# Five layer norms: the apply goes from VectorE to ScalarE, epsilon and shift to GpSimd

## The chip, the cores and the metric

The kernel runs on one core of one Trainium2 chip. Its engines are TensorE (PE in the profile, with weight loads as PEld), VectorE (DVE), ScalarE (ACT), GpSimd (POOL) and SyncE (SP, which here only issues transfers). The metric is the time of one execution on the device in microseconds; lower is better.

## The reference

The inputs are 32 sequences of 128 tokens with 256 features, `x`, and as many context tokens. The block is a gated decoder layer and a gated feed-forward:

```python
x = x + tanh(g_xattn) * xattn(layernorm(x), ctx)      # norm 0 is this layernorm
x = x + tanh(g_ffn) * ffn(layernorm(x))               # norm 4

def xattn(x, ctx):
    x = ln(x + mha(x, x, x))        # norm 1, with gain and bias; 16 heads of 16
    x = ln(x + mha(x, ctx, ctx))    # norm 2
    f = relu(x @ w1 + b1) @ w2 + b2
    return ln(x + f)                # norm 3

def layernorm(x): return (x - mean(x)) / sqrt(var(x) + 1e-5)
```

`ffn` is a SiLU-gated product with ternary weights, whose input is rounded to 8 bits by the maximum of each token's row. Each norm is taken over the 256 features of a token.

## The kernel before

The 32 sequences go in 16 groups of two (`G = 2` slots b), each slot a tile of 128 tokens by 256 features. A group passes five stages, each in another iteration of one software pipeline: `Ap` and `A` (self attention, norms 0 and 1), `Bp` and `B` (cross attention, norm 2), `C` (the inner feed-forward, norm 3) and `E` (the ternary one, norm 4). One iteration therefore works on several groups at once, and 20 iterations do all. Iterations 0 to 4 are written out, 5 to 15 are a loop, and the rest are written out again. In the first three the ternary weights are also prepared.

`SCHEDULE` is one list of steps that all engines walk through. Each engine issues its own part of a step at that step's place, in order, and waits on semaphores for what others must do first. An engine therefore can't pass a step whose input is late, though the next one may be ready. The stretches that matter here read, in the schedule's words:

- `("O", -1), ("E", "norm"), ("W", -1), ("smax", 1, 2), ("in", "B", "K"), ("N", -1), ("Bp", "Q"), ("E", "TQ")`: norm 4 of one group stands between output steps of stage B. `W` is the output projection with the residual and the statistics of norm 1 or 2, `N` its apply.
- `("E", "GU", 0, 2), ("Ap", "norm"), ("scores", 0, 1), ("M", 1)`: norm 0 of a new group stands ahead of the scores of an attention unit. `scores` on ACT is two exponentials (`e` in float32, `ehi` in float16), on POOL their difference `elo`; `M` sends the row maxima, as `mT`, through a transfer into `stk`, whose last rows then take part in the score products.
- `("scores", 3, 1), ("smax", 4, 3), ("E", "DN", 1, 2), ("W", 2), ("M", 4), ("C", "apply"), ("Ap", "V"), ("setup", 3), ("N", 2)`: the end of an iteration. `smax` takes row maxima (`nm`) on DVE.

Queries and keys leave for DRAM (`parts`) and come back in another layout (`stk`), by transfers that SP issues; TensorE's `smax` steps wait for them. SP too goes in order: at `("Ap", "norm")` it waits for norm 0 before it loads the next `x_a`, and the transfer of `mT` stands behind that.

A norm n goes, before: DVE takes `bn_stats` and `bn_aggr` (mean and variance in `lmv`), then adds epsilon (`lve`); POOL raises that to -0.5 (`lrs`); DVE subtracts the mean and multiplies by `lrs` in one instruction for each slot (`normalize`). For norms 1 to 3 POOL then multiplies by the gain (`tg`) and adds the bias (`h`).

Of the kernel before, what the change touches and what calls it, by code (L numbers as in the profile page):

```python
# [30 lines left out]
P = 128  # L31
# [170 lines left out]
def build(nc, x, ctx_in, mask_x, mask_s, g_x, g_f, w, out):  # L202
    with ExitStack() as stack:
# [3 lines left out]
        def sem(name):  # L207
            return stack.enter_context(nc.semaphore(name))
# [143 lines left out]
        ln_aggr = {n: sem(f"ln_aggr{n}") for n in range(5)}  # L352
        ln_eps = {n: sem(f"ln_eps{n}") for n in range(5)}
        ln_rstd = {n: sem(f"ln_rstd{n}") for n in range(5)}
        ln_out = {n: sem(f"ln_out{n}") for n in range(5)}
# [66 lines left out]

        N_CONST = 12
        N_DVE = 15
# [373 lines left out]
        def _(eng):  # L798
# [19 lines left out]
            def ternary(m, part):  # L818
# [6 lines left out]
                if part == 1:  # L825
                    eng.wait_ge(u_tc, 7 * m + 3)
                    eng.activation(tq[:, :], raw[10 + m], ACT.Identity, scale=sw[:, m:m + 1], bias=magic_col[:, 0:1]).then_inc(u_tq, 1)

            def prep(st_, s, name):
                g = st_.g[{"A": "Ap", "B": "Bp"}.get(s, s)]  # L830
                if name == "norm":

                    eng.wait_ge(q_small, g.at(5, 5))
                    wait(eng, *st_.full("E", "TQ", back=1))
                    for b in range(G):
                        a_ = eng.activation(q1m[:, b, :], h4[:, b, :], ACT.Identity, scale=s1[:, b:b + 1],  # L836
                                            bias=magic_col[:, 0:1])
                    a_.then_inc(q_ready, 1)
                    return
# [49 lines left out]
            def unit_step(st_, what, k, hf=0):  # L889
                s, b, g, turn = st_.unit(k)  # L890
                if what == "scores":
# [15 lines left out]
            def iteration(st_):  # L907
                for step in SCHEDULE:
# [6 lines left out]
                    if what in ("scores", "M", "O"):  # L915
                        unit_step(st_, *step)
                    elif name in ("GU", "DN", "Q2"):
                        beside(st_, *step)
                    elif what in STAGE and name not in ("F2", "stats", "apply") and step != ("Ap", "norm"):
                        prep(st_, STAGE[what], name)  # L920
# [14 lines left out]
        def _(eng):  # L935
# [98 lines left out]
            def stats(n, g, calls, call, slots, src):  # L1034

                for k in slots:
# [6 lines left out]
                i_.then_inc(ln_aggr[n], 1)  # L1043
                eng.wait_ge(ln_aggr[n], g.at(calls, call + 1))
                a, b = slots[0], slots[-1] + 1
                eng.tensor_scalar(lve[n][:, a:b], lmv[n][:, a:b, 1], EPS, None, ALU.add).then_inc(ln_eps[n], 1)  # L1046

            def normalize(n, g, calls, call, slots, src, dst):
                eng.wait_ge(ln_rstd[n], g.at(calls, call + 1))
                for k in slots:  # L1050
                    i_ = eng.tensor_scalar(dst(k), src(k), lmv[n][:, k, 0:1], lrs[n][:, k:k + 1], ALU.subtract, ALU.mult)  # L1051
                i_.then_inc(ln_out[n], 1)

            def first_norm(st_):
# [3 lines left out]
                wait(eng, *st_.full("A", "T", back=1))  # L1058
                wait(eng, hres_in["A"], g.at(16))
                normalize(0, g, 1, 0, range(G), lambda k: x_a[:, k, :], lambda k: hin["A"][:, k, :])  # L1060

            def prep(st_, s, name):
                g = st_.g[{"A": "Ap", "B": "Bp"}.get(s, s)]
                if name == "norm":

                    eng.wait_ge(x1_ready, g.at(1, 1))
                    stats(4, g, 1, 0, range(G), lambda j: x1[:, j, :])
                    wait(eng, q_ready, g.at(1))
                    normalize(4, g, 1, 0, range(G), lambda j: x1[:, j, :], lambda j: h4[:, j, :])
                    eng.wait_ge(ln_out[4], g.at(1, 1))  # L1070
# [43 lines left out]
            def unit_step(st_, what, k, part=0):  # L1114
# [30 lines left out]
                elif what == "W":  # L1145

                    bank, fill, drain, before, after = st_.job(s, ("W", k))
                    eng.wait_ge(fill, after)
                    eng.wait_ge(hres_in[s], g.at(16, 16))
                    eng.scalar_tensor_tensor(res[s][:, b, :], bank[:, 0:D], 1.0 / WS, hres[s][:, b, :], ALU.mult,  # L1150
                                             ALU.add).then_inc(drain, 1)
                    eng.wait_ge(drain, after)
                    stats(LN_OF[s], g, G, b, range(b, b + 1), lambda i: res[s][:, i, :])
                elif what == "N":
                    wait(eng, ln_gain[LN_OF[s]], g.at(G, b))
                    normalize(LN_OF[s], g, G, b, range(b, b + 1), lambda i: res[s][:, i, :], lambda i: nrm[s][:, i, :])

            def beside(st_, s, kind, k=0, j=0):
                g = st_.g[s]
                if kind == "F2":  # L1160
                    bank, fill, drain, before, after = st_.job("C", ("F2", k))
                    eng.wait_ge(fill, after)
                    eng.wait_ge(ln_bias[2], g.at(G, k + 1))
                    eng.scalar_tensor_tensor(res["C"][:, k, :], bank[:, 0:D], 1.0 / (WS * WS), hin["C"][:, k, :],
                                             ALU.mult, ALU.add).then_inc(drain, 1)
# [3 lines left out]
                if kind == "apply":  # L1169
                    wait(eng, ln_gain[3], g.at(1))  # L1170
                    normalize(3, g, 1, 0, range(G), lambda j: res["C"][:, j, :], lambda j: nrm["C"][:, j, :])
                if kind == "GU":
# [32 lines left out]
            def iteration(st_):  # L1205
                for step in SCHEDULE:
# [6 lines left out]
                    if what in ("smax", "values", "O", "W", "N"):  # L1213
                        unit_step(st_, *step)
                    elif step == ("Ap", "norm"):
                        first_norm(st_)
                    elif name in ("F2", "stats", "apply", "GU", "DN", "Q2"):
                        beside(st_, *step)
# [15 lines left out]
        def _(eng):  # L1234
# [14 lines left out]
            const(eng.memset(ones16[:, :], 1.0))  # L1249
            const(eng.memset(neghalf[:, :], -0.5))  # L1250
            const(eng.memset(magic_col[:, :], MAGIC))
            const(eng.memset(brows[:, :], 0.0))
# [123 lines left out]
```

## Time and profile before

| | |
|---|---|
| time, median of 3 runs | 1311.1 us (1307.93 to 1313.27) |
| profiled execution, span | 1305.9 us (its time outside the span isn't recorded) |
| busy: TensorE, DVE, ACT, POOL | 72%, 69%, 43%, 42% of the span |
| mean granted TensorE clock | 0.880 |

The span is from the first to the last instruction of the one execution that the profiler recorded. A busy share is a mean over the whole span. All other times of this document that are no medians are read from that execution.

### The profile page before, as it was taken

How to read it: one execution, taken by the hardware profiler on the slowest of the kernel's cores; microseconds unless marked ns; L12 is line 12 of the kernel's file. 1: busy time of each engine (PE TensorE's matmuls, PEld its weight loads, DVE VectorE, ACT ScalarE, POOL GpSimd, SP SyncE). 2: the span in 40 equal slices, each digit the busy share in tenths (PEclk: the TensorE clock that was granted, in tenths of full speed). 3: DMA queues.
4: the chain of work that ended last, by engine and by line, in shares of the span. 5: the costliest groups of instructions: out<-in, count | busy, mean ns of one | idle time of the engine just before them, and what ended most of it. 6: DMA issues, size and time to landing. Idle time of an engine off the chain costs nothing.

```text
span 1305.9 us, 28843 instructions
## 1 busy us (share of the span) xinstructions
PE 941.4 (72%) x10103; PEld 737.1 (56%) x10147; DVE 902.5 (69%) x2063; ACT 561.7 (43%) x836; POOL 549.1 (42%) x468
## 2 busy tenths in 40 slices
PE   1254567868778787878787778797878778786674
PEld 1133445646666665656665657575756666564452
DVE  8544356558787877787878788686868787666544
ACT  2212243435444554545455445453535454542432
POOL 5012134453535454444536354535453545460510
PEclk9866677979898989898999999898999898988886
DMA  4523442424444444453544425243534444404000
GB/s 139 121 81 49 78 55 42 84 40 77 64 74 75 73 73 73 57 89 53 93 53 78 64 68 75 54 81 55 86 48 76 65 65 74 66 10 66 17 9 8
DMA packets 136288, 85.07 MB, mean 65 GB/s; under 512 B 10632, under 2 KB 131631, under 8 KB 136240
## 3 DMA queue, kind: packets, MB, share of 16 engines
q1 hardware_dynamic: 136240, 84.43, 38.2%
q8 instruction: 31, 0.51, 0.2%
q14 instruction: 17, 0.14, 0.1%
HBM read 54.49 MB, written 20.98 MB: 58 GB/s over the span
## 4 chain that ended last, share of the span: by engine, by line
PE 27%; DVE 21%; DMA 18%; issue 16%; POOL 10%; ACT 4%; SPq 3%; DVEq 1%; POOLq 0%; ACTq 0%
DMA stk_AQ<-parts_AQ 9%; PE lin_A L583 4%; PE lin_E L583 3%; DMA parts_AQ<-qk_AQ 3%; DMA stk_BQ<-parts_BQ 3%; PE lin_B L583 3%; PE smax L659 3%; SPq L476 3%; POOL lrs L1268 2%; DVE nm_A L1119 2%; PE smax L655 2%; PE st L685 2%; DMA parts_BQ<-qk_BQ 2%; PE lin_B L752 2%; DMA stk_AQ<-mT_A 2%
## 5 line engine op out<-in xcount | busy, mean ns | idle before, releaser
L1283 POOL TENSOR_TENSOR elo<-e,ehi 128x1024 f16<-128x1024 f32 x128 | 272.6, 2130 | 303.4 <-ACT ehi L896 302.8
L894 ACT ACTIVATE e<-st 128x1024 f32<-128x1024 f32 x128 | 131.0, 1024 | 190.5 <-PE st L685 190.4
L1268 POOL TENSOR_TENSOR lrs<-lve,neghalf 128x1 f32<-128x1 f32 (+1 forms) x112 | 70.0, 625 | 333.8 <-DVE lve L1046 332.2
L1119 DVE TENSOR_REDUCE nm_A<-smax 128x4 f32<-128x512 f32 x128 | 87.8, 686 | 81.3 <-PE smax L659 80.9
L896 ACT ACTIVATE ehi<-st 128x1024 f16<-128x1024 f32 x128 | 130.9, 1022 | 0.0
L655 PE MATMUL smax<-mb,ident_big 128*128 128x512 f16 x128 | 57.6, 450 | 101.5 <-DMA stk_AQ<-parts_AQ 73.7
L1119 DVE TENSOR_REDUCE nm_B<-smax 128x4 f32<-128x512 f32 x128 | 87.7, 685 | 20.1 <-PE smax L659 19.8
L659 PE MATMUL smax<-stk_BK,stk_BQ 126*128 126x128 f16 x512 | 51.7, 225 | 45.2 <-DMA stk_BQ<-parts_BQ 40.9
L655 PEld LDWEIGHTS smax<-mb,ident_big 128*128 128x128 f16 x128 | 13.2, 103 | 112.8 <-issue 54.2
L659 PEld LDWEIGHTS smax<-stk_BK,stk_BQ 126*128 126x128 f16 x512 | 35.1, 100 | 60.3 <-issue 24.7
L875 ACT ACTIVATE late<-late,magic_col,s 128x1024 f32<-128x1024 f32 x32 | 39.7, 1240 | 60.8 <-DVE s L1195 60.8
L680 PE MATMUL st<-mbT,ident_big 128*128 128x512 f16 x128 | 54.0, 422 | 6.0 <-DMA stk_AQ<-mT_A 5.1
L659 PEld LDWEIGHTS smax<-stk_AK,stk_AQ 126*128 126x128 f16 x512 | 45.9, 110 | 21.7 <-issue 10.4
L659 PE MATMUL smax<-stk_AK,stk_AQ 126*128 126x128 f16 x512 | 57.9, 243 | 0.0
L836 ACT ACTIVATE late<-late,magic_col,s 128x256 f32<-128x256 f32 x32 | 17.5, 592 | 90.5 <-DVE kap L1080 90.5
L685 PEld LDWEIGHTS st<-stk_AQ,stk_AK 128*128 128x128 f16 x512 | 43.2, 106 | 21.3 <-issue 7.4
L685 PE MATMUL st<-stk_AQ,stk_AK 128*128 128x128 f16 x512 | 53.6, 231 | 0.0
L583 PE MATMUL lin_E<-hT_C,w 128*128 128x256 f16 x384 | 50.6, 272 | 0.0
L619 PE MATMUL lin_E<-ident,late 128*128 128x128 f32 x64 | 12.2, 321 | 51.2 <-ACT late L836 51.2
L699 PE MATMUL av<-vhi_B,ehi 128*128 128x17 f16 x512 | 45.6, 172 | 3.0 <-POOL elo L1283 3.0
L1051 DVE TENSOR_SCALAR h<-x_a,lmv,lrs 128x256 f32<-128x256 f32 x32 | 37.4, 1209 | 14.5 <-POOL lrs L1268 14.5
L685 PE MATMUL st<-stk_BQ,stk_BK 128*128 128x128 f16 x512 | 44.5, 237 | 2.6 <-DVE mw L1011 1.3
(281 smaller groups left out, 3006.0 us busy)
## 6 DMA issues: line engine op xcount, KB each, us to landing
stk_AK<-parts_AK SPq DMA_DIRECT2D x64, 128.0 KB, 4.7
stk_AQ<-parts_AQ SPq DMA_DIRECT2D x64, 128.0 KB, 7.0
stk_BK<-parts_BK SPq DMA_DIRECT2D x64, 128.0 KB, 4.4
stk_BQ<-parts_BQ SPq DMA_DIRECT2D x64, 128.0 KB, 4.6
x_a<-in_x_dram SPq DMA_DIRECT2D x16, 256.0 KB, 2.8
cx<-in_ctx_dram SPq DMA_DIRECT2D x16, 256.0 KB, 2.8
parts_AK<-qk_AK SPq DMA_DIRECT2D x16, 256.0 KB, 2.3
parts_AQ<-qk_AQ SPq DMA_DIRECT2D x16, 256.0 KB, 2.9
```

The costliest lines, as they stand in the source:

```text
L583: mm = eng.matmul(dst, lhs(a, k), rhs(b, k), start=(start and at == 0), stop=(at == last))
L655: eng.matmul(smax[:, :], ident_big[:, :], mb[:, :].unsqueeze(1).to_broadcast([P, 4, P]), start=True, stop=True)
L659: mm = eng.matmul(smax[:, i * P:(i + 1) * P], stk[s, "Q"][0:XROW, h, tok], stk[s, "K"][0:XROW, h, tok], start=(s == "B"), stop=True, skip_ ...
L680: eng.matmul(st[:, k2 * 512:(k2 + 1) * 512], ident_big[:, :], mbT[:, :].unsqueeze(1).to_broadcast([P, 4, P]), start=True, stop=True)
L685: mm = eng.matmul(st[:, col:col + P], stk[s, "K"][:, h, tok], stk[s, "Q"][:, h, tok], start=(s == "B"), stop=True, skip_group_check=True)
L699: eng.matmul(dst, ehi[:, hf, i * P:(i + 1) * P], vhi[s][:, b, h, :], start=True, stop=False, skip_group_check=True)
L875: eng.activation(q2m[:, :], z2[:, :], ACT.Identity, scale=s2[:, 0:1], bias=magic_col[:, 0:1]).then_inc(q2_ready, 1)
L894: eng.activation(e32[:, hf, :], st[:, :], ACT.Exp, scale=SCORE).then_inc(e32_ready, 1)
L896: eng.activation(ehi[:, hf, :], st[:, :], ACT.Exp, scale=SCORE).then_inc(st_drained, 1)
L1119: eng.tensor_reduce(nm[s][:, 4 * part:4 * part + 4], smax[:, :].rearrange("p (h k) -> p h k", h=4), AX_X, ALU.max, negate=True).then_inc(s ...
L1268: eng.tensor_tensor(lrs[n][:, a:b], lve[n][:, a:b], neghalf[:, 0:b - a], ALU.pow).then_inc(ln_rstd[n], 1)
L1283: eng.tensor_tensor(elo[:, hf, :], e32[:, hf, :], ehi[:, hf, :], ALU.subtract).then_inc(elo_ready, 1)
```

## The change

Three pieces of a norm move, for all five norms:

- DVE keeps `bn_stats` and `bn_aggr` only. The epsilon step goes to POOL as a `tensor_tensor` add with a column of epsilons.
- POOL takes four dependent steps where it took one: epsilon (`lve`), power (`lrs`), mean times `lrs` (`lmr`), and that times -1 (`lnm`), each waiting for the one before through a semaphore.
- The apply becomes an ACT instruction, scale `lrs` and bias `lnm`, at the step's place in ACT's order.

Added waits keep a new set of statistics or a new residual from overwriting what the last apply still reads. The pieces of the diff below are, in order: the new columns, ScalarE, VectorE, GpSimd.

```diff
+        negone = sb("negone", [P, 4], F32)
+        eps_col = sb("eps_col", [P, 4], F32)
...
+            def normalize(n, g, calls, call, slots, src, dst):
+                eng.wait_ge(ln_rstd[n], g.at(calls, call + 1))
+                for k in slots:
+                    i_ = eng.activation(dst(k), src(k), ACT.Identity, scale=lrs[n][:, k:k + 1], bias=lnm[n][:, k:k + 1])
+                i_.then_inc(ln_out[n], 1)
...
+                if name == "norm" and s == "A":
+                    wait(eng, *st_.full("A", "T", back=1))
+                    wait(eng, hres_in["A"], g.at(16))
+                    normalize(0, g, 1, 0, range(G), lambda k: x_a[:, k, :], lambda k: hin["A"][:, k, :])
+                    return
                 if name == "norm":
-
+                    wait(eng, q_ready, g.at(1))
+                    normalize(4, g, 1, 0, range(G), lambda j: x1[:, j, :], lambda j: h4[:, j, :])
                     eng.wait_ge(q_small, g.at(5, 5))
...
+                if kind == "apply":
+                    wait(eng, ln_gain[3], g.at(1))
+                    normalize(3, g, 1, 0, range(G), lambda j: res["C"][:, j, :], lambda j: nrm["C"][:, j, :])
+                    return
...
+                elif what == "N":
+                    wait(eng, ln_gain[LN_OF[s]], g.at(G, b))
+                    normalize(LN_OF[s], g, G, b, range(b, b + 1), lambda i: res[s][:, i, :], lambda i: nrm[s][:, i, :])
...
             def stats(n, g, calls, call, slots, src):
-
+                wait(eng, ln_rstd[n], g.back(1).at(calls, call + 1))
...
-                eng.wait_ge(ln_aggr[n], g.at(calls, call + 1))
-                a, b = slots[0], slots[-1] + 1
-                eng.tensor_scalar(lve[n][:, a:b], lmv[n][:, a:b, 1], EPS, None, ALU.add).then_inc(ln_eps[n], 1)
-
-            def normalize(n, g, calls, call, slots, src, dst):
-                eng.wait_ge(ln_rstd[n], g.at(calls, call + 1))
-                for k in slots:
-                    i_ = eng.tensor_scalar(dst(k), src(k), lmv[n][:, k, 0:1], lrs[n][:, k:k + 1], ALU.subtract, ALU.mult)
-                i_.then_inc(ln_out[n], 1)
...
             def power(n, g, calls, call, slots):
 
+                eng.wait_ge(ln_aggr[n], g.at(calls, call + 1))
+                a, b = slots[0], slots[-1] + 1
+                eng.tensor_tensor(lve[n][:, a:b], lmv[n][:, a:b, 1], eps_col[:, 0:b - a], ALU.add).then_inc(ln_eps[n], 1)
                 eng.wait_ge(ln_eps[n], g.at(calls, call + 1))
-                a, b = slots[0], slots[-1] + 1
-                eng.tensor_tensor(lrs[n][:, a:b], lve[n][:, a:b], neghalf[:, 0:b - a], ALU.pow).then_inc(ln_rstd[n], 1)
+                eng.tensor_tensor(lrs[n][:, a:b], lve[n][:, a:b], neghalf[:, 0:b - a], ALU.pow).then_inc(ln_pow[n], 1)
+                eng.wait_ge(ln_pow[n], g.at(calls, call + 1))
+                eng.tensor_tensor(lmr[n][:, a:b], lmv[n][:, a:b, 0], lrs[n][:, a:b], ALU.mult).then_inc(ln_shift[n], 1)
+                eng.wait_ge(ln_shift[n], g.at(calls, call + 1))
+                eng.tensor_tensor(lnm[n][:, a:b], lmr[n][:, a:b], negone[:, 0:b - a], ALU.mult).then_inc(ln_rstd[n], 1)
```

What stands in a row now is shown at three places. A row is a line of the kernel, an operation, what it writes and reads, and its shape.

On ACT in iteration 4, from the norm of stage E to the maxima of the next unit, there stood before (`late<-late,magic_col,s` is the 8-bit rounding `q1m`, `late<-lin_E,hcg` a tanh of the gate):

```order
L836 ACTIVATE late<-late,magic_col,s 128x256 x2
L866 ACTIVATE qk_BQ<-lin_B 128x512
L843 ACTIVATE q1T<-lin_E 128x512
L883 ACTIVATE late<-lin_E,hcg 128x512
L866 ACTIVATE hT_C<-lin_B 128x512
L883 ACTIVATE late<-lin_C,hcg 128x512
L894 ACTIVATE e<-st 128x1024
L896 ACTIVATE ehi<-st 128x1024
L901 ACTIVATE mT_A<-lin_A 32x128
```

and now:

```order
L838 ACTIVATE late<-late,lnm,lrs 128x256 x2
L854 ACTIVATE late<-late,magic_col,s 128x256 x2
L838 ACTIVATE nrm_B<-res_B,lnm,lrs 128x256
L884 ACTIVATE qk_BQ<-lin_B 128x512
L861 ACTIVATE q1T<-lin_E 128x512
L905 ACTIVATE late<-lin_E,hcg 128x512
L884 ACTIVATE hT_C<-lin_B 128x512
L905 ACTIVATE late<-lin_C,hcg 128x512
L838 ACTIVATE h<-x_a,lnm,lrs 128x256 x2
L916 ACTIVATE e<-st 128x1024
L918 ACTIVATE ehi<-st 128x1024
L926 ACTIVATE mT_A<-lin_A 32x128
```

Three applies came in: that of norm 4 ahead of the rounding, that of norm 2 between the rounding and the copies `qk_BQ` and `q1T`, and that of norm 0 between a tanh and the exponentials `e` and `ehi`.

On POOL in the same stretch, from the split of the keys of B to the next `elo`, there stood before:

```order
L1274 TENSOR_TENSOR qk_BK<-qf_B,qk_BK 128x512
L1268 TENSOR_TENSOR lrs<-lve,neghalf 128x2
L1268 TENSOR_TENSOR lrs<-lve,neghalf 128x1
L1290 TENSOR_TENSOR tg_B<-nrm_B,lng 128x256
L1298 TENSOR_TENSOR h<-tg_B,lnb 128x256
L1268 TENSOR_TENSOR lrs<-lve,neghalf 128x2
```

and now:

```order
L1293 TENSOR_TENSOR qk_BK<-qf_B,qk_BK 128x512
L1281 TENSOR_TENSOR lve<-lmv,eps_col 128x2
L1283 TENSOR_TENSOR lrs<-lve,neghalf 128x2
L1285 TENSOR_TENSOR lmr<-lmv,lrs 128x2
L1287 TENSOR_TENSOR lnm<-lmr,negone 128x2
L1281 TENSOR_TENSOR lve<-lmv,eps_col 128x1
L1283 TENSOR_TENSOR lrs<-lve,neghalf 128x1
L1285 TENSOR_TENSOR lmr<-lmv,lrs 128x1
L1287 TENSOR_TENSOR lnm<-lmr,negone 128x1
L1309 TENSOR_TENSOR tg_B<-nrm_B,lng 128x256
L1317 TENSOR_TENSOR h<-tg_B,lnb 128x256
L1281 TENSOR_TENSOR lve<-lmv,eps_col 128x2
```

Each single power became four steps; nothing else changed places.

On DVE at the end of an iteration, between two row maxima `nm_A`, there stood before:

```order
L1138 TENSOR_TENSOR o_B<-av,rsum 128x256
L1051 TENSOR_SCALAR nrm_A<-res_A,lmv,lrs 128x256
L1119 TENSOR_REDUCE nm_A<-smax 128x4
L1143 TENSOR_TENSOR oT_B<-lin_B,oT_B 128x256
L1119 TENSOR_REDUCE nm_A<-smax 128x4
L1126 TENSOR_SCALAR nm_A<-nm_A 128x16
```

The row of L1051 is gone there, and with it all others of that line on DVE.

## Rows read from the trace of the kernel before

**Rows 1.** The page, section 1: busy time, share of the span, instructions.

```profile
PE 941.4 (72%) x10103; PEld 737.1 (56%) x10147; DVE 902.5 (69%) x2063; ACT 561.7 (43%) x836; POOL 549.1 (42%) x468
```

**Rows 2.** Timeline of TensorE, three waits for `stk_AQ`: start, length, [idle before <-releaser].

```profile
267.16 0.61 PE L655 MATMUL smax<-mb,ident_big 128*128 128x512 f16 x1 [5.81 <-DMA stk_AQ<-parts_AQ]
...
680.25 0.39 PE L655 MATMUL smax<-mb,ident_big 128*128 128x512 f16 x1 [4.34 <-DMA stk_AQ<-parts_AQ]
...
1092.31 0.60 PE L655 MATMUL smax<-mb,ident_big 128*128 128x512 f16 x1 [4.30 <-DMA stk_AQ<-parts_AQ]
```

**Rows 3.** Timeline of TensorE, DVE and POOL, 617 to 628 us, by start.

```profile
617.16 0.39 PE L659 MATMUL smax<-stk_AK,stk_AQ 126*128 126x128 f16 x4
617.30 2.34 DVE L1051 TENSOR_SCALAR nrm_A<-res_A,lmv,lrs 128x256 f32<-128x256 f32 x1
617.36 2.13 POOL L1283 TENSOR_TENSOR elo<-e,ehi 128x1024 f16<-128x1024 f32 x1 [0.95 <-ACT ehi L896]
...
619.56 0.68 DVE L1119 TENSOR_REDUCE nm_A<-smax 128x4 f32<-128x512 f32 x1
...
621.20 2.12 POOL L1283 TENSOR_TENSOR elo<-e,ehi 128x1024 f16<-128x1024 f32 x1
...
623.62 0.23 PE L669 MATMUL lin_C<-ident,nm_A 128*32 128x128 f16 x1 [1.07 <-DVE nm_A L1128]
...
627.44 0.68 DVE L1090 TENSOR_TENSOR hT_B<-lin_E,hT_B 128x512 f16<-128x512 f32 x1
```

**Rows 4.** Groups by line and shape: busy us, mean ns of one, idle before.

```profile
L1268 POOL TENSOR_TENSOR lrs<-lve,neghalf 128x1 f32<-128x1 f32 x64 | 35.9, 561 | 209.9 <-DVE lve L1046 209.9
L1268 POOL TENSOR_TENSOR lrs<-lve,neghalf 128x2 f32<-128x2 f32 x48 | 34.0, 709 | 123.9 <-DVE lve L1046 122.4
...
L1290 POOL TENSOR_TENSOR tg_A<-nrm_A,lng 128x256 f32<-128x256 f32 x32 | 23.2, 725 | 12.8 <-DVE nrm_A L1051 12.8
...
L1307 POOL TENSOR_TENSOR late<-late,lng 128x512 f32<-128x512 f32 x16 | 20.3, 1267 | 2.7 <-DVE late L1051 2.7
...
L836 ACT ACTIVATE late<-late,magic_col,s 128x256 f32<-128x256 f32 x32 | 17.5, 592 | 90.5 <-DVE kap L1080 90.5
...
L1250 POOL MEMSET neghalf<- 128x4 f32 x1 | 0.1, 101 | 0.1
```

**Rows 5.** Timeline of DVE, POOL and ACT, 636 to 641 us, by start.

```profile
636.12 0.73 DVE L1051 TENSOR_SCALAR late<-late,lmv,lrs 128x256 f32<-128x256 f32 x2 [0.89 <-POOL lrs L1268]
...
638.48 1.09 ACT L836 ACTIVATE late<-late,magic_col,s 128x256 f32<-128x256 f32 x2 [5.29 <-DVE kap L1080]
...
639.27 0.18 DVE L1042 BATCH_NORM_AGGREGATE lmv<-lst 128x2 f32<-128x6 f32 x1
...
639.72 0.54 POOL L1268 TENSOR_TENSOR lrs<-lve,neghalf 128x1 f32<-128x1 f32 x1 [3.71 <-DVE lve L1046]
...
640.37 0.41 DVE L1051 TENSOR_SCALAR nrm_B<-res_B,lmv,lrs 128x256 f32<-128x256 f32 x1
...
640.77 0.60 ACT L843 ACTIVATE q1T<-lin_E 128x512 bf16<-128x512 f32 x1 [0.72 <-PE lin_E L619]
```

**Rows 6.** Timeline of ACT, DVE, TensorE and SP, 645 to 654 us, by start.

```profile
645.15 1.02 ACT L894 ACTIVATE e<-st 128x1024 f32<-128x1024 f32 x1 [0.21 <-PE st L685]
...
646.78 0.15 DVE L1042 BATCH_NORM_AGGREGATE lmv<-lst 128x2 f32<-128x6 f32 x1
646.97 0.25 ACT L901 ACTIVATE mT_A<-lin_A 32x128 f16<-32x128 f16 x1
...
648.03 2.45 DVE L1051 TENSOR_SCALAR h<-x_a,lmv,lrs 128x256 f32<-128x256 f32 x2 [0.90 <-POOL lrs L1268]
...
651.02 0.40 PE L659 MATMUL smax<-stk_BK,stk_BQ 126*128 126x128 f16 x4 [2.06 <-DMA stk_BQ<-parts_BQ]
651.19 0.72 SPq L489 DMA_DIRECT2D stk_AQ<-mT_A  x1
...
653.76 0.39 PE L680 MATMUL st<-mbT,ident_big 128*128 128x512 f16 x1 [0.36 <-DMA stk_AQ<-mT_A]
```

More of the change, by code:

```diff
@@ L325, in build @@
         lrs = [sb(f"lrs{n}", [P, G], F32) for n in range(5)]
+        lnm = [sb(f"lnm{n}", [P, G], F32) for n in range(5)]
+        lmr = [sb(f"lmr{n}", [P, G], F32) for n in range(5)]
         carrier = sb("carrier", [1, 1], F32)
@@ L353, in build @@
         ln_eps = {n: sem(f"ln_eps{n}") for n in range(5)}
+        ln_pow = {n: sem(f"ln_pow{n}") for n in range(5)}
+        ln_shift = {n: sem(f"ln_shift{n}") for n in range(5)}
         ln_rstd = {n: sem(f"ln_rstd{n}") for n in range(5)}
@@ L914, in iteration @@
                         continue
-                    if what in ("scores", "M", "O"):
+                    if what in ("scores", "M", "O", "N"):
                         unit_step(st_, *step)
@@ L918, in iteration @@
                         beside(st_, *step)
-                    elif what in STAGE and name not in ("F2", "stats", "apply") and step != ("Ap", "norm"):
+                    elif name == "apply":
+                        beside(st_, *step, 0)
+                    elif what in STAGE and name not in ("F2", "stats"):
                         prep(st_, STAGE[what], name)
@@ L1057, in first_norm @@
                 stats(0, g, 1, 0, range(G), lambda k: x_a[:, k, :])
-                wait(eng, *st_.full("A", "T", back=1))
-                wait(eng, hres_in["A"], g.at(16))
-                normalize(0, g, 1, 0, range(G), lambda k: x_a[:, k, :], lambda k: hin["A"][:, k, :])
             def prep(st_, s, name):
@@ L1067, in prep @@
                     stats(4, g, 1, 0, range(G), lambda j: x1[:, j, :])
-                    wait(eng, q_ready, g.at(1))
-                    normalize(4, g, 1, 0, range(G), lambda j: x1[:, j, :], lambda j: h4[:, j, :])
                     eng.wait_ge(ln_out[4], g.at(1, 1))
@@ L1149, in unit_step @@
                     eng.wait_ge(hres_in[s], g.at(16, 16))
+                    wait(eng, ln_out[LN_OF[s]], g.back(1).at(G, b + 1))
                     eng.scalar_tensor_tensor(res[s][:, b, :], bank[:, 0:D], 1.0 / WS, hres[s][:, b, :], ALU.mult,
@@ L1153, in unit_step @@
                     stats(LN_OF[s], g, G, b, range(b, b + 1), lambda i: res[s][:, i, :])
-                elif what == "N":
-                    wait(eng, ln_gain[LN_OF[s]], g.at(G, b))
-                    normalize(LN_OF[s], g, G, b, range(b, b + 1), lambda i: res[s][:, i, :], lambda i: nrm[s][:, i, :])
             def beside(st_, s, kind, k=0, j=0):
@@ L1163, in beside @@
                     eng.wait_ge(ln_bias[2], g.at(G, k + 1))
+                    wait(eng, ln_out[3], g.at(1))
                     eng.scalar_tensor_tensor(res["C"][:, k, :], bank[:, 0:D], 1.0 / (WS * WS), hin["C"][:, k, :],
@@ L1168, in beside @@
                     stats(3, g, 1, 0, range(G), lambda b: res["C"][:, b, :])
-                if kind == "apply":
-                    wait(eng, ln_gain[3], g.at(1))
-                    normalize(3, g, 1, 0, range(G), lambda j: res["C"][:, j, :], lambda j: nrm["C"][:, j, :])
                 if kind == "GU":
@@ L1212, in iteration @@
                         continue
-                    if what in ("smax", "values", "O", "W", "N"):
+                    if what in ("smax", "values", "O", "W"):
                         unit_step(st_, *step)
@@ L1216, in iteration @@
                         first_norm(st_)
-                    elif name in ("F2", "stats", "apply", "GU", "DN", "Q2"):
+                    elif what == "N" or name == "apply":
+                        continue
+                    elif name in ("F2", "stats", "GU", "DN", "Q2"):
                         beside(st_, *step)
@@ L1250, in _ @@
             const(eng.memset(neghalf[:, :], -0.5))
+            const(eng.memset(negone[:, :], -1.0))
+            const(eng.memset(eps_col[:, :], EPS))
             const(eng.memset(magic_col[:, :], MAGIC))
```

2 lines of the change are left out of this document (1 added, 1 removed).

## The prediction

> **What bounds the kernel now.** I read the page's first section, then the TensorE waits on a transfer, then the timeline of one period engine by engine. The first shows that no engine is full: TensorE 941.4 us of 1305.9, VectorE (DVE) 902.5, ScalarE (ACT) 561.7, GpSimd (POOL) 549.1 [rows 1]. The bound is a chain through queues that each run in a written order. The second shows its beat: once a period TensorE waits some 4.3 us for the transfer of `stk_AQ`. From 267.16 to 1092.31 there are 12 such periods, (1092.31 - 267.16) / 12 = 68.8 us each [rows 2]. That wait is resolved by a DMA that itself answers to work earlier in the period, so whatever delays the middle of a period delays the next one's start. I follow one period, from 610 to 680 us.
>
> **Prices.** Removed from DVE: 160 applies (5 norms, 16 groups, 2 slots) and 112 epsilon adds. An apply is 0.41 us when nothing disturbs it, a pair 0.73 [rows 5], but 2.34 us at 617.30 and 2.45 a pair at 648.03 [rows 3, 6]: in rows 3 it began at 617.30, POOL's `elo` ran 617.36 to 619.49, and it ended at 619.64. Added to ACT: the same applies. The nearest row is `q1m`, also 128x256 with two column operands, 0.592 us [rows 4] and 1.09 for a pair [rows 5], so one costs 0.18 more than on DVE, a pair 0.36 more, and the next ACT instruction starts 0.50 after each.
>
> Added to POOL: three small steps per call beside the power. No row shows a small add or multiply there. Below, the cheapest POOL instruction, a memset of four columns, is 0.10; above, the power itself is 0.56 on one column [rows 4]. Between them the straight line through its products, 0.725 at 256 columns and 1.267 at 512, meets zero columns at 0.725 - 0.542 = 0.18. I take 0.20, because that row is the same instruction with a cheap operation. The hand-over between two dependent POOL instructions I estimate at 0.13 (bounds 0.08 and 0.17).
>
> The chain from the aggregate to the scale was: aggregate ends 639.27 + 0.18 = 639.45, power starts 639.72, so 0.27 for the DVE epsilon and its hand-overs [rows 5]. New: a hand-over of 0.10, then three times (0.20 + 0.13), so 1.09. Each norm's chain grows by X = 1.09 - 0.27 = 0.82 us (bounds 0.10 + 3 x 0.18 - 0.27 = 0.37 and 0.10 + 3 x 0.73 - 0.27 = 2.02).
>
> **The sum over one period.** First what is won. Without `nrm_A` at 617.30 the row maximum that starts at 619.56 can start at about 617.6, when its product is done (617.16 + 0.39), and the max transposes of 623.62 come about 2 us earlier [rows 3]. Half of that is lost at once: `nrm_B` now stands on ACT ahead of the copy of `hT_B`, and its scale waits for POOL's `elo`, which ends at 621.20 + 2.12 = 623.32. Then hand-over 0.10, epsilon 0.20, power 0.56 and two more small steps with three hand-overs of 0.13: 624.97. ACT applies at 625.07, the copy starts 0.50 later and ends at 626.17, and DVE's half of `hT_B` starts at 626.2 where it started at 627.44 [rows 3]. Gain 1.25 us, which the next steps (keys, values, output of B) carry, since each waits for the one before.
>
> Then what is paid. (a) The norm ahead of the feed-forward, on two slots: X + 0.36 = 1.18. So `q1m` moves from 638.48 to 638.48 - 1.25 + 1.18 = 638.41 [rows 5]. (b) `nrm_B` of that place stands on ACT between `q1m` and the copies `qk_BQ` and `q1T`. Its aggregate ends at 639.45 - 0.07 = 639.38; 0.10 + 0.20 + 0.13 + 0.56 + 0.13 + 0.20 + 0.13 + 0.20, and 0.10 to reach ACT, is 1.75: 641.13. Two starts of 0.50 later `q1T` starts at 642.13, where it started at 640.77 [rows 5]: the period is now 1.36 late, and TensorE's gate and up products behind it. (c) The norm of `x_a` follows these on DVE: its aggregate ends at 646.93 + 1.36 = 648.29. The chain on two columns (power 0.709 [rows 4]) takes 1.80, and 0.10 to ACT: 650.19. There the pair stands ahead of the exponentials `e` and `ehi` of another unit, which need nothing from it: `e` starts 1.0 later, at 651.19 instead of 645.15, and `mT_A`, 1.82 behind it (646.97 - 645.15), at 653.01 [rows 6]. Before, the transfer that carries `mT_A` was held on SP behind the load of `x_a`, which waits for this very norm (648.03 + 2.45 = 650.48), and was issued at 651.19. Now the norm ends at 651.3, but `mT_A` at 653.26, and the transfer goes at about 653.3. The scores waited 653.76 - 651.19 = 2.57 for it, so they start at 655.9: 2.1 us late [rows 6]. Queued behind the held ACT instructions are also the two feed-forward copies and `hT_A`; all are done before the late scores, so they add nothing.
>
> From there to the next `stk_AQ` wait no norm is on the path (`nrm_A` of the other slot costs ACT 0.5 us shortly ahead of TensorE's wait of 4.3, which absorbs it), so I let the 2.1 us stand. 12 x 2.1 = 25 us. At the ends I count +5 us, an estimate: the first norm and the last four feed-forward norms pay 1.18 each (5.9), the drain's two B applies about 1.0 each, and the relief of 1.25 comes back in two of its iterations; in the fill I let relief and stall cancel. In all +30: 1305.9 + 30 = 1336 us of span. The profiled execution shows its span alone; the median of the runs is 1311.1, so 5.2 us lie around it or are scatter, and the forecast for the median is **1341 us**.
>
> A rule that bears on the relief: the Trainium skill, "SBUF — State Buffer", section "SBUF: two separate sides", says that GpSimd and a VectorE instruction that uses both ports of the shared pair exclude each other for a whole instruction. The end of `nrm_A` 0.15 us behind `elo` agrees [rows 3]. If instead whatever DVE does next were held as long, the 1.25 us would be lost and the period 3.3 us late: 12 x 3.3 + 5 = 45, so 1356 us.
>
> **Rivals.** *The relief carries, and the waits on ACT are covered (faster).* For it: TensorE waits 2.06 us for `stk_BQ` at 651.02 in this stretch, and the old `x_a` norm took 2.45 us on DVE [rows 6]. Then every period keeps the 1.25: -15 + 5 = -10, 1301 us. It decides where `mT_A` leaves ACT by 651.19 - 1.25 = 649.9, so with the pair started by 646.9. Against it: even with the whole relief the aggregate ends at 645.7 and the chain gives 647.5.
>
> *It evens out.* With X at its lower bound the four chains of a period give back 4 x 0.45 = 1.8 of the 2.1: 12 x 0.3 + 2, so 1317 us. For it speaks only the memset.
>
> *A small POOL step costs what the power costs.* X = 2.02, so 4 x 1.2 = 4.8 more per period: 12 x 6.9 + 12 = 95, 1406 us. For it: the two rows on one and two columns are 0.561 and 0.709, and both are mostly fixed time [rows 4]. Against it: at that fixed time 256 columns could not take 0.725.
>
> **How the numbers follow.** Measured runs of this kernel spread over 0.4%, so about 0.5% (6.6 us) can be told from no change. Chances: the forecast, 1318 to 1365, 0.63; dear POOL steps, above 1365, 0.12; evened out, within 6.6 us, 0.10; relief carried, faster, 0.15. So faster 0.15, same 0.10, slower 0.75. The range 1304 to 1385 leaves out most of the faster case and the far half of the dear one.
>
> **What would show it.** Of the changed kernel: DVE busy below 780 us (902.5 - 160 x 0.41 - stretches); ACT near 650 us; small POOL steps near 0.2 us; between `tanh` and `e` on ACT a wait of some 4 us for the shift of `x_a`; a period near 71 us; `nrm_A` gone from the gap between two row maxima. I am wrong if the small steps cost over 0.4 us, if the 2 us won near 618 us reach the period's end, or if TensorE's granted clock falls in the longer waits.

## The result, and the profile after

| | before | after |
|---|---|---|
| time, median | 1309.5 us (1301.9 to 1313.3, 4 runs) | 1331.3 us (1330.1 to 1334.4, 4 runs) |
| span of the profiled execution | 1305.9 us | 1332.6 us |
| mean granted TensorE clock | 0.880 | 0.868 |

The change makes the kernel slower: the ratio is 1.0175, with a 95% interval of 1.0128 to 1.0221. Forecast were 1341 us and slower.

The page's first section of the changed kernel, which answers to [rows 1]:

```profile
PE 950.0 (71%) x10103; PEld 742.0 (56%) x10147; DVE 760.7 (57%) x1791; ACT 638.4 (48%) x996; POOL 610.0 (46%) x806
```

DVE lost 142 us of work (902.5 to 760.7), ACT gained 77, POOL 61, and TensorE is busy almost as long as before. The span grew all the same: the freed engine was not the bound.

TensorE's wait for `stk_AQ` in the timeline of the changed kernel, answering to [rows 2]:

```profile
265.70 0.61 PE L661 MATMUL smax<-mb,ident_big 128*128 128x512 f16 x1 [6.29 <-DMA stk_AQ<-parts_AQ]
...
1112.71 0.58 PE L661 MATMUL smax<-mb,ident_big 128*128 128x512 f16 x1 [4.23 <-DMA stk_AQ<-parts_AQ]
```

Twelve periods lie between the two rows: (1112.71 - 265.70) / 12 = 70.58 us each, where it was 68.76. So the 26.7 us of span are 12 x 1.82 = 21.8 in the periods, -1.5 ahead of the first row (267.16 before), and +6.3 behind the last (1332.6 - 1112.71 = 219.9, before 1305.9 - 1092.31 = 213.6).

The prices, from POOL's and ACT's groups by line and shape (busy us, mean ns of one, idle before), answering to [rows 4]:

```profile
L1283 POOL TENSOR_TENSOR lrs<-lve,neghalf 128x1 f32<-128x1 f32 x64 | 34.7, 543 | 5.0
...
L1285 POOL TENSOR_TENSOR lmr<-lmv,lrs 128x1 f32<-128x1 f32 x64 | 12.1, 190 | 5.0
L1281 POOL TENSOR_TENSOR lve<-lmv,eps_col 128x1 f32<-128x1 f32 x64 | 12.1, 190 | 188.4 <-DVE lmv L1069 188.4
```

```profile
L838 ACT ACTIVATE nrm_B<-res_B,lnm,lrs 128x256 f32<-128x256 f32 x32 | 19.2, 600 | 47.0 <-POOL lnm L1287 47.0
L838 ACT ACTIVATE h<-x_a,lnm,lrs 128x256 f32<-128x256 f32 x32 | 17.5, 593 | 66.3 <-POOL lnm L1287 66.3
```

A small POOL step costs 0.19 us, an ACT apply 0.60. The idle time in the last column says where ACT now stands still: 66.3 us in all ahead of the norm of `x_a`, 47.0 ahead of `nrm_B`, both waiting for POOL's last step. ACT's timeline of one such place, answering to [rows 6]:

```profile
727.95 1.09 ACT L838 ACTIVATE h<-x_a,lnm,lrs 128x256 f32<-128x256 f32 x2 [3.31 <-POOL lnm L1287]
728.94 1.00 ACT L916 ACTIVATE e<-st 128x1024 f32<-128x1024 f32 x1
729.85 1.01 ACT L918 ACTIVATE ehi<-st 128x1024 f16<-128x1024 f32 x1
730.75 0.25 ACT L926 ACTIVATE mT_A<-lin_A 32x128 f16<-32x128 f16 x1
```

The two exponentials and the copy of `mT_A` queue behind the applies of `h`, as forecast.

One period is a poor guide here, so the tables below are means over ten: a period begins where SP issues the transfer `parts_AQ<-qk_AQ`, the last ten intervals between such issues are taken (from 66.8 to 70.1 us in the kernel before), and a number is the mean start of the instruction behind that issue. They are worked out from the timelines of the engines.

```
mean start in the period, us                 before   after   difference
first row maximum behind stk_AQ (DVE)         13.27   13.27      0.00
third row maximum (DVE)                       20.23   19.17     -1.06
copy of the first mT_A (ACT)                  24.13   23.43     -0.70
hT_B, DVE's half                              27.96   27.51     -0.45
maximum behind norm 4 (DVE)                   37.34   37.76     +0.42
q1T (ACT)                                     40.85   42.84     +1.99
e queued behind h (ACT)                       45.61   52.15     +6.54
transfer of the second mT_A (SP)              51.32   54.24     +2.92
e of the scores that need it (ACT)            55.32   57.53     +2.21
period                                        68.59   70.81     +2.22
```

The column on the right is the forecast's walk through a period, measured: a gain at the row maxima that shrinks, three losses, and nothing after the scores.

### The profile page after: what moved, and what is told of

Read it like the earlier page. It is cut to its first block, busy times and chain, and to the rows that moved or that the text cites. A ratio compares the mean times of both kernels' runs of the same rounds, so it can differ in the third digit from the quotient of the medians.

```text
span 1332.6 us, 29220 instructions
## 1 busy us (share of the span) xinstructions
PE 950.0 (71%) x10103; PEld 742.0 (56%) x10147; DVE 760.7 (57%) x1791; ACT 638.4 (48%) x996; POOL 610.0 (46%) x806
## 4 chain that ended last, share of the span: by engine, by line
PE 28%; DMA 17%; DVE 16%; POOL 15%; issue 12%; ACT 10%; SPq 2%; ACTq 0%; DVEq 0%; POOLq 0%
DMA stk_AQ<-parts_AQ 9%; POOL elo L1302 5%; PE lin_A L589 4%; POOL lrs L1283 3%; PE lin_E L589 3%; DMA parts_AQ<-qk_AQ 3%; PE lin_B L589 2%; SPq L482 2%; PE smax L665 2%; DMA stk_AQ<-mT_A 2%; DVE lst L1064 2%; DMA stk_BQ<-parts_BQ 2%; PE st L691 2%; PE lin_B L758 2%; ACT ehi L918 1%
## 5 line engine op out<-in xcount | busy, mean ns | idle before, releaser
L1281 POOL TENSOR_TENSOR lve<-lmv,eps_col 128x1 f32<-128x1 f32 (+1 forms) x112 | 21.4, 191 | 312.8 <-DVE lmv L1069 312.6
L838 ACT ACTIVATE late<-late,lnm,lrs 128x256 f32<-128x256 f32 x64 | 34.8, 592 | 62.2 <-POOL lnm L1287 62.2
L1123 DVE SCALAR_TENSOR_TENSOR late<-lin_B,late 128x512 f16<-128x512 f32 x16 | 11.1, 692 | 73.9 <-ACT late L884 73.9
L838 ACT ACTIVATE h<-x_a,lnm,lrs 128x256 f32<-128x256 f32 x32 | 17.5, 593 | 66.3 <-POOL lnm L1287 66.3
```

Of the source, the lines that this page charges most:

```text
L838: i_ = eng.activation(dst(k), src(k), ACT.Identity, scale=lrs[n][:, k:k + 1], bias=lnm[n][:, k:k + 1])
```

## The experiments

Behind each run stands the ratio of its time to the kernel before on the same chip, with its 95% interval.

### One norm at a time

`APPLY` chooses for each norm how it is done: "act" as in the changed kernel, "dve" as before. Against the changed kernel, for `only_norm1`:

```diff
+APPLY = {0: "dve", 1: "act", 2: "dve", 3: "dve", 4: "dve"}
+ON_ACT = ("act", "bare")
+ON_POOL = ("act", "chain")
...
+        zero_col = sb("zero_col", [P, 4], F32)
...
+                shift = zero_col if APPLY[n] == "bare" else lnm[n]
...
-                elif what == "N":
+                elif what == "N" and APPLY[LN_OF[s]] in ON_ACT:
...
+                if APPLY[n] not in ON_POOL:
+                    eng.wait_ge(ln_aggr[n], g.at(calls, call + 1))
+                    a, b = slots[0], slots[-1] + 1
+                    eng.tensor_scalar(lve[n][:, a:b], lmv[n][:, a:b, 1], EPS, None, ALU.add).then_inc(ln_eps[n], 1)
```

> Only the norm of A (`nrm_A`) is applied by ScalarE with its four steps on GpSimd; the other four stay as in the kernel before. Theory (the loss comes from applies that stand in ScalarE's queue ahead of work that needs nothing from them; nrm_A has nothing urgent behind it): the row maxima no longer have nrm_A between them, the max transposes come some 0.7 to 0.8 us earlier as in the changed kernel, and no nrm_B holds the copy of hT_B, so the 0.8 carries: period about 68.0 instead of 68.8, time 8 to 12 us shorter. Rival 1 (what is won near the row maxima is lost at the next wait): no change, within 3 us. Rival 2 (the longer GpSimd chain costs wherever it stands): 5 to 10 us longer.

> Only the norm of x_a is applied by ScalarE, the other four as before. Theory (as predicted in step c): the pair stands ahead of e and ehi on ScalarE, e some 4 us later, mT_A leaves ScalarE 4.4 us later, but its transfer was held by the load of x_a anyway until 39.1 us after the period's start, so it goes about 0.8 us later: period +0.8, time 8 to 12 us longer. Rival 1 (this norm alone made the loss of the changed kernel, and the others even out): 22 us or more longer. Rival 2 (the transfer is hidden, as the DVE apply of 2.45 us is gone): no change.

> Only the norm ahead of the feed-forward is applied by ScalarE, the other four as before. Theory: the absolute maximum behind it comes later by the chain and the two applies, measured as +0.94 us in the changed kernel (from -0.49 to +0.45 against before), and q1T, the feed-forward products and the scores follow it: period +0.9, time 10 to 14 us longer. Rival (a wait of TensorE later in the period hides it): within 3 us.

> Only the norm of B (`nrm_B`) and the last norm (C) are applied by ScalarE, the others as before. Theory: nrm_B stands on ScalarE ahead of the copy of hT_B, and at its second place ahead of qk_BQ and q1T; without the relief from nrm_A the first costs up to 1.0 us (aggregate 13.1 us after the period's start, chain 1.85, copy at 15.5 instead of 13.7, of which DVE's half of hT_B shows 1.0), the second 1.5 as in the changed kernel: period +2 to +2.5, time 25 to 32 us longer, the dearest of the four runs. Rival (norm 0 is the dear one, and these two have slack): under 10 us longer.

Measured: norm 1 alone 1232.6 us (0.9407, 0.9344 to 0.9470), norm 0 alone 1258.5 (0.9614, 0.9548 to 0.9679), norm 4 alone 1269.8 (0.9691, 0.9627 to 0.9755), norms 2 and 3 1277.7 (0.9740, 0.9668 to 0.9813). All four are faster than the kernel before on the same chip, by 31 to 76 us. Neither theory nor any rival had that, though the order of the four is the theory's. Something that the four share and neither kernel has must be worth some 60 us. The list of transfers (count, KB each, median us from issue to landing) showed it; of the kernel before:

```profile
stk_AK<-parts_AK SPq DMA_DIRECT2D x64, 128.0 KB, 4.7
stk_AQ<-parts_AQ SPq DMA_DIRECT2D x64, 128.0 KB, 7.0
stk_BK<-parts_BK SPq DMA_DIRECT2D x64, 128.0 KB, 4.4
stk_BQ<-parts_BQ SPq DMA_DIRECT2D x64, 128.0 KB, 4.6
```

and of `only_norm1`:

```profile
stk_AK<-parts_AK SPq DMA_DIRECT2D x64, 128.0 KB, 4.0
stk_AQ<-parts_AQ SPq DMA_DIRECT2D x64, 128.0 KB, 5.6
stk_BK<-parts_BK SPq DMA_DIRECT2D x64, 128.0 KB, 3.8
stk_BQ<-parts_BQ SPq DMA_DIRECT2D x64, 128.0 KB, 3.7
```

The transfer at the head of every period lands 1.4 us earlier, with the same bytes. My switch had brought one more constant column, `zero_col`, and so moved every tile allocated after it by 32 bytes.

### The addresses

Four kernels move tiles by an unused one and change no instruction; a fifth takes the column out again:

```diff
         neghalf = sb("neghalf", [P, 4], F32)
+        pad = sb("pad", [P, 8], F32)
```

(`[P, 24]` for 96 bytes; behind `eps_col` in the changed kernel.) For the `stk` tiles alone:

```diff
+        pad = sb("pad", [P, 8], F32)
         stk = {(s, t): sb(f"stk_{s}{t}", [P, NH, T], F16) for s in "AB" for t in "QK"}
+        pad2 = sb("pad2", [P, 8], F32)
```

and for `only_norm1_old_addresses`, against `only_norm1`:

```diff
-        zero_col = sb("zero_col", [P, 4], F32)
...
-                shift = zero_col if APPLY[n] == "bare" else lnm[n]
+                shift = lnm[n]
```

> The kernel before with one unused tile of 32 bytes a partition after neghalf, so that all later tiles (x_a to the end, the stk tiles among them) begin at multiples of 64 bytes instead of 32 above one; no instruction is changed. The four runs of single norms all held one more 16-byte column than the changed kernel, which moves these tiles in the same way, and in them the transfers stk_AQ<-parts_AQ landed in 5.5 to 5.6 us instead of 7.0. Theory (those four runs were faster by the address, not by the norms): transfers as short as there, some 1245 to 1255 us, so that against it the single norms stand at about -15 (norm 1), +8 (norm 0), +20 (norm 4), +28 (norms 2 and 3). Rival (ScalarE's applies made them faster): 1309 us, as before.

> The changed kernel with the same unused tile of 32 bytes, so that it stands at the same addresses modulo 64 as the kernel in the run beside this one. Theory (the change costs the same at either address): 22 to 26 us above that run, so about 1270 us, against 1331 at the addresses that it had. Rival 1 (the addresses have nothing to do with it): 1331. Rival 2 (with faster transfers other waits end last, and the norms on ScalarE cost nothing): equal to the run beside it within 5 us.

> The kernel before with 32 unused bytes ahead of the four stk tiles and 32 behind them: only these four begin at multiples of 64 bytes, all other tiles after them and before them lie as in the kernel before modulo 64. Theory (what gets faster is the transfers that write the stk tiles): as fast as the run with every tile moved, within 6 us. Rival (other transfers, of x_a and hres and of mT, or the engines' own reads and writes carry it): less than half of that gain.

> Only the norm of A on ScalarE, now without the extra 16-byte column, so that all tiles lie as in the changed kernel modulo 64. Theory (address and norm act apart): 8 to 14 us below the kernel before, 1296 to 1301 us. Rival 1 (the relief is lost at the next wait): within 3 us of before. Rival 2 (no address effect): 1233 us as in the run with the extra column.

> The kernel before with an unused tile of 96 bytes a partition after neghalf: stk_AQ begins at byte 148736, a multiple of 128, as in the runs of single norms and in the changed kernel with 32 bytes more (before: 148640, 32 above a multiple of 128; with 32 bytes: 64 above one). No instruction is changed. Theory (the transfers that write the stk tiles depend on the start modulo 128: 7.0 us at 32 and 96, 6.5 at 64, 5.5 at 0): stk_AQ lands in 5.5 to 5.6 us and the time is 1240 to 1255 us, so that the single norms stand near -15, +8, +20, +28 us against it and the whole change at +30 to +45. Rival (at equal addresses the norms on ScalarE are themselves the gain, and 128 gives nothing over 64): 1285 to 1292 us, as with 32 bytes.

The last of these five was written when the times of the other four were known.

Measured: before with 32 bytes 1291.8 us (0.9853, 0.9806 to 0.9900); the `stk` tiles alone 1293.3 (0.9857, 0.9814 to 0.9900); before with 96 bytes 1250.0 (0.9526, 0.9468 to 0.9585); the changed kernel with 32 bytes 1285.1 (0.9790, 0.9747 to 0.9833); norm 1 alone at the old addresses 1291.1 (0.9842, 0.9797 to 0.9886).

The 32 bytes gave the kernel before only a third of what I expected: it was not yet at the address of the four runs, since my rule went by multiples of 64 bytes alone. With 96 it was, and the time is inside the expected range. The changed kernel with 32 bytes stands at that address too, so its neighbour is the run with 96, and against it the change costs 35 us (1285.1 - 1250.0). At the old addresses it cost 22 (1331.3 - 1309.5). The run that moves only the `stk` tiles gains as much as the one that moves all, so at 32 bytes it is these tiles; at 96 they were not moved alone. The list of transfers of before with 32 bytes, then with 96:

```profile
stk_AQ<-parts_AQ SPq DMA_DIRECT2D x64, 128.0 KB, 6.5
```

```profile
stk_AQ<-parts_AQ SPq DMA_DIRECT2D x64, 128.0 KB, 5.6
stk_BK<-parts_BK SPq DMA_DIRECT2D x64, 128.0 KB, 3.8
```

With 96 bytes the first row maximum of a period starts at 10.89 us instead of 13.27, and the period is 65.11 us instead of 68.59: two thirds of the gain arise at that one transfer. The changed kernel had left these transfers as slow as they were before, by the place of its own new columns.

With this the single norms can be read, against 1250.0 at equal addresses: norm 1 alone -17, norm 0 alone +8, norm 4 alone +20, norms 2 and 3 +28, all five +35. These runs were made on different chips, each beside the kernel before on its own; by the ratios instead of the times the five are -16, +12, +22, +28 and +35. The intervals of norm 1 and of the kernel with 96 bytes just touch, and that of norm 0 overlaps the latter, so a loss by norm 0 alone is not clear. The run of norm 1 at the old addresses needs no such bridge: it gains 1.6% (1.1 to 2.0), more than the 8 to 14 us expected. Norm 4 costs more than the 10 to 14 expected.

### The chain against the place

At equal addresses, the two halves of the change apart: the long chain with DVE's apply, and the short chain with ACT's. The edit is `APPLY` alone ("chain" and "bare" for all five). In the second the shift is a column of zeros, so it leaves out the subtraction of the mean.

> All five norms with their four steps on GpSimd as in the changed kernel, but applied by VectorE as before (with mean and scale, the shift is computed and not used). Addresses modulo 128 as in the run of 96 bytes. Theory (what the change loses is half the longer chain, +0.8 us a norm, and half the place of the applies in ScalarE's queue; what it wins is nrm_A out of VectorE's row maxima, which this run does not have): 15 to 30 us above the run of 96 bytes. Rival 1 (ScalarE's queue makes all of the loss): within 5 us of the run of 96 bytes. Rival 2 (the chain makes all of it): as much above that run as the changed kernel with 32 bytes more, which took 1285, or more.

> All five norms applied by ScalarE, but with the chain of before: VectorE adds epsilon, GpSimd takes the power and nothing else. The shift is a column of zeros, so the subtraction of the mean is left out. Addresses modulo 128 as in the runs that took 1250 (all as before), 1297 (long chain, VectorE applies) and 1285 (long chain, ScalarE applies): this is the fourth corner. Theory after those three (the longer chain costs about 47 us and the place of the applies gains about 12, and the two act apart): 1233 to 1245 us. Rival 1 (ScalarE's queue costs too, and only hid behind the chain): 1255 or more. Rival 2 (without the chain the relief of all applies is far larger): 1225 or less.

Measured 1297.4 us (0.9879, 0.9850 to 0.9909) and 1246.8 (0.9507, 0.9462 to 0.9551). The four corners:

```
us                              VectorE applies   ScalarE applies
epsilon on DVE, power on POOL        1250.0            1246.8
four steps on POOL                   1297.4            1285.1
```

The longer chain makes the loss: 47 us with DVE's applies, 38 with ACT's. Whether by its own length or by holding POOL's queue longer is not separated. The move of the applies to ACT costs nothing in sum: it gives 12 us beside the long chain, and 3, which is inside the scatter, beside the short one. TensorE's granted clock differs between the corners: in the ten periods used below it is 0.98 with 96 bytes and 0.94 with the long chain on DVE, but 0.92 in both kernels with ACT's applies. So the 38 us are measured at equal clocks, the 47 are not. Rival 2 of the first run is the one that held, my half-and-half theory fell; in the second run the time lies 2 us above the theory's range, and neither rival fits. Mean starts at equal addresses show how (us in the period, and the difference to the first column):

```
                                  +96 bytes   all five on ACT     short chain on ACT
hT_B, DVE's half                    25.06       24.81  -0.25        23.74  -1.32
maximum behind norm 4               34.45       35.06  +0.61        33.40  -1.05
q1T                                 37.90       40.14  +2.24        37.88  -0.02
e queued behind h                   42.56       49.40  +6.84        46.59  +4.03
transfer of the second mT_A         48.31       51.49  +3.18        48.68  +0.37
e of the scores that need it        51.83       54.69  +2.86        51.88  +0.05
period                              65.11       67.96  +2.85        65.15  +0.04
```

(The second column is the changed kernel with 32 bytes.) With the short chain, ACT's applies win 1.32 us at `hT_B` and lose 0.27 at norm 4 and 1.03 at the `nrm_B` ahead of `q1T`, which levels out. `e` still stands behind `h` and is 4 us late, but that costs only 0.07 at the scores: the transfer of `mT_A` had been held almost as long by the load of `x_a` (47.86 in the kernel with 96 bytes, the transfer at 48.31). The long chain then adds 1.07, 0.59, 0.60 and 0.55 us at the four places (second column against third), 2.81 a period.

One reason why the long chain may be dearer on DVE than on ACT is seen in two timelines of `gpsimd_steps_dve_apply`, of POOL and of DVE; the fall of the clock from 0.98 to 0.94 is another, and no run separates them:

```profile
881.39 0.19 POOL L1330 TENSOR_TENSOR lnm<-lmr,negone 128x1 f32<-128x1 f32 x1
881.53 2.13 POOL L1345 TENSOR_TENSOR elo<-e,ehi 128x1024 f16<-128x1024 f32 x1
```

```profile
881.68 2.13 DVE L1089 TENSOR_SCALAR nrm_A<-res_A,lmv,lrs 128x256 f32<-128x256 f32 x1 [0.19 <-POOL lnm L1330]
883.73 0.68 DVE L1159 TENSOR_REDUCE nm_A<-smax 128x4 f32<-128x512 f32 x1
```

POOL's last step releases DVE's apply and, in POOL's own order, is followed by `elo` at once. The apply starts 0.15 us into it and ends 0.15 us behind it. This `nrm_A`, between the row maxima, took over 1.7 us in 15 of 16 groups here, in 10 of 16 in the kernel with 96 bytes and in 8 of 16 in the kernel before. The Trainium skill, "SBUF — State Buffer", section "SBUF: two separate sides", says of a VectorE instruction in a 2-port mode and a GpSimd instruction that whichever starts first holds the shared ports for its whole instruction. The two rows agree, with an apply of 2.13 us for one of 0.41; no run shows the apply's mode, and a start a little ahead of `elo` was not enough, as the last section shows.

### The step of norm 0 moved

Against the changed kernel's order, all else as in `APPLY` with "act" for all five:

```diff
-    ("Ap", "norm"), ("scores", 0, 1), ("M", 1), ("values", 0, 0), ("C", ("F", 0)), ("C", ("F", 1)),
+    ("scores", 0, 1), ("M", 1), ("Ap", "norm"), ("values", 0, 0), ("C", ("F", 0)), ("C", ("F", 1)),
```

> The changed kernel, with the step of the norm of x_a moved on all engines behind the scores of the next unit and the max transposes that follow it, so that e, ehi and the copy of mT_A stand ahead of its two applies on ScalarE. Addresses modulo 128 as in the changed kernel with 32 bytes more (1285 us). Theory (step c of the prediction: e and mT_A wait on ScalarE for a norm that they don't need): mT_A leaves ScalarE some 4 us earlier, but TensorE comes to the scores late by q1T anyway and waited only 0.5 us for mT_A in the changed kernel: 1275 to 1281. Rival 1 (norm 0 is the main loss): 1265 or less. Rival 2 (the load of x_a, which the moved norm releases later, is missed by the next step): slower than 1285.

Measured 1306.6 us (0.9953, 0.9933 to 0.9973), 21 us above the changed kernel at the same addresses. It is slower, as rival 2 had it, but not through the load that it named. TensorE's waits (us in total, times, longest):

```profile
PE lin_E L629 <- ACT late L862: 67.2, 16, 11.4
PE lin_C L623 <- ACT h L843: 53.1, 15, 13.4
```

and in the changed kernel with 32 bytes:

```profile
PE lin_C L620 <- ACT h L839: 16.0, 3, 13.4
PE st L687 <- DMA stk_AQ<-mT_A: 7.2, 13, 2.7
```

The wait for the second `mT_A` (7.2 us in all) is gone, and in its place TensorE waits 53.1 us instead of 16.0 for `h` itself, whose transposes follow a few steps later. One such wait in its timeline:

```profile
643.34 1.12 PE L623 MATMUL lin_C<-ident,h 128*128 128x128 f32 x4 [2.83 <-ACT h L843]
```

So ACT's order can't be mended by this exchange: one of the two is late either way.

## Why the prediction was right, step by step

**The bound and the beat** held. The beat is the `stk_AQ` wait, still 4.2 to 4.6 us in the later periods, and what delays a period's middle delays its end: 12 x 1.82 - 1.5 + 6.3 = +26.7 against 12 x 2.1 + 5 = +30. For the median the forecast put another 5.2 us around the span. In the profiled run of the changed kernel only 1.8 lie there (1334.4 - 1332.6), so the rest was scatter of the runs before.

**Small POOL steps**: 0.20 forecast, 0.19 measured; the dear rival is out. **X**, the longer chain: 0.82 forecast. POOL's steps of one `nrm_B`, whose aggregate ends at 717.13 + 0.18 = 717.31:

```profile
717.39 0.19 POOL L1281 TENSOR_TENSOR lve<-lmv,eps_col 128x1 f32<-128x1 f32 x1 [3.88 <-DVE lmv L1069]
717.65 0.54 POOL L1283 TENSOR_TENSOR lrs<-lve,neghalf 128x1 f32<-128x1 f32 x1
718.27 0.19 POOL L1285 TENSOR_TENSOR lmr<-lmv,lrs 128x1 f32<-128x1 f32 x1
718.54 0.19 POOL L1287 TENSOR_TENSOR lnm<-lmr,negone 128x1 f32<-128x1 f32 x1
```

ACT's apply starts at 718.76, 1.45 us behind the aggregate, where DVE's started 0.92 behind (640.37 - 639.45) [rows 5]. X was 0.53 here: the hand-overs between POOL's steps are 0.08 instead of 0.13, and ACT starts 0.03 behind the last step instead of 0.10.

**The relief at the row maxima** was forecast as 1.25 us at `hT_B` and was 0.45. This is the term that was mis-sized. I read it from one period in which `nrm_A` took 2.34 us [rows 3]. It was stretched in 8 of 16 groups. In the others it took 0.41: `elo` didn't run beside it, or began 0.11 to 0.29 us after it, as in these rows of the kernel before, of DVE and of POOL:

```profile
825.69 0.40 DVE L1051 TENSOR_SCALAR nrm_A<-res_A,lmv,lrs 128x256 f32<-128x256 f32 x1
```

```profile
825.91 2.17 POOL L1283 TENSOR_TENSOR elo<-e,ehi 128x1024 f16<-128x1024 f32 x1 [0.95 <-ACT ehi L896]
```

The third row maximum came 1.06 us earlier in the mean, not 2.0.

**The three losses**: (a) norm 4, 1.18 forecast, 0.87 measured (from -0.45 to +0.42). (b) `nrm_B` ahead of `q1T`, 1.43 forecast (from -0.07 to +1.36), 1.57 measured. (c) norm 0, 0.74 forecast (from 1.36 to 2.1), 0.22 measured. The transfer of `mT_A` was 2.92 late, the scores only 2.21. The sum, 2.1 against 2.2 in these ten periods, is that close by luck: 0.80 too much relief and 0.69 too much loss stood against each other.

In (b) the forecast let TensorE wait for `q1T`. Ahead of the first gate product, shown further down, DVE's half of `qk_BQ` came last in 11 of 16 groups (19.8 us of its idle time), `q1T` in 5 (9.3). Both stand behind `nrm_B` on ACT, the first through ACT's copy `qk_BQ`.

**The weight given to the place in (c)** did not hold. The words of (c) put its loss down to `e` and `mT_A` standing behind a norm that they don't need. With the short chain that place costs 0.07 us, and another place for the norm cost 21 us in the whole. At equal addresses the step from `q1T` to the scores is 0.62 with the long chain (2.86 - 2.24).

**The chain's share** was in the sum: four chains a period, each longer by X = 0.82, are 3.3 us, and the rest of the sum gives back 1.2. At equal addresses, with ACT's applies, the long chain adds 2.81 us a period; the move of the applies, with the short chain, adds 0.04 and gives nothing back. So what turns the change into a loss is the length of the chain, at all four places.

**Of the signs named**, DVE below 780 us (760.7), ACT near 650 (638.4), POOL steps near 0.2, a wait of some 4 us ahead of `h` (3.31 in the row shown with the result, 4.1 in the mean, 66.3 / 16), a period near 71 us and `nrm_A` gone from between the maxima all came. TensorE's clock, named as a way to be wrong, fell a little: 0.880 to 0.868 in the mean, 0.94 to 0.91 in the ten periods. The first gate product, which reads the late `q1T`, took 518 ns before and 633 after, in the groups by line of before and of after:

```profile
L742 PE MATMUL lin_E<-wgT,q1T 128*128 128x512 bf16 x16 | 8.3, 518 | 7.9 <-ACT q1T L843 7.1 <-issue 0.6 <-DVE qk_BQ L1103 0.2
```

```profile
L748 PE MATMUL lin_E<-wgT,q1T 128*128 128x512 bf16 x16 | 10.1, 633 | 29.2 <-DVE qk_BQ L1116 19.8 <-ACT q1T L861 9.3
```

Before, 9 of these 16 products began at the clock's upper level (2.4 GHz); after, all 16 ran at the lower one (1.2 GHz), each behind 1.2 to 2.7 us in which TensorE stood idle (29.2 us in all instead of 7.9). No run here separates the clock's share of the loss. A gain is there for norm 1 alone: 1232.6 us, the fastest of all kernels here, 6% below before, of which 4.7% is the address. Its expectation put that down to nothing urgent standing behind `nrm_A` on ACT; the runs show the gain, not the reason.

What stays open: why norm 4 alone costs 20 us and not 12. Its `nrm_A`, still on DVE, was stretched in 11 of 16 groups, against 10 at the same addresses without the change, which is too little to explain it.

## What to carry to other kernels

Moving an apply off a busy engine is worth what its end releases: read how long the chain from statistics to apply becomes, and count over all periods, not in one, how often two engines hold each other up. An edit that adds or removes a small tile moves every later one, so compare variants at equal addresses, and try an unused pad ahead of tiles that transfers write in small pieces.

## What the runs showed of the hardware

**A transfer's landing depends on where its target begins.** The transfers from `parts` write the four `stk` tiles in pieces of 512 bytes (256 float16). `stk_AQ` began at byte 148640 of a partition before, 148704 in the changed kernel, 148672 with 32 bytes and 148736 with 96. That is 160, 224, 192 and 0 above a multiple of 256, and its transfers landed after 7.0, 6.9, 6.5 and 5.6 us (medians). A start 128 above such a multiple was not tried, so the runs can't tell 128 from 256, and "modulo 128" in the expectations claims more than they show. The kernel before took 1309.5 us at the first, 1291.8 at 192 and 1250.0 at 0. The Trainium skill, "DMA: Bandwidth & Descriptors", section "How a descriptor splits into AXI transactions", says of reads that a descriptor that doesn't begin at a multiple of 256 bytes starts with a transaction at the boundary below. The traces agree in direction for these writes into SBUF; they don't show the mechanism.

**A DVE apply beside POOL's `elo`.** Eight kernels here keep `nrm_A` on DVE. In them it overlapped `elo` 113 times. In 87 of these it began inside `elo` or up to 0.09 us ahead of it, and took 1.7 to 2.4 us, until 0.15 behind `elo`'s end; one is that of [rows 3], 0.06 ahead. In 26 it began 0.10 us or more ahead, and took its 0.41. So by the recorded starts, being first by less than 0.1 us was not enough.

**A POOL step of one column** costs 0.19 us with a cheap operation and 0.54 with the power, and 0.08 us lie between two dependent ones.
